# A decoder layer on one core: x loaded once into its final place, cross-attention scores as two halves of 64 rows

## The reference

```
x = ln(x + attn(x))          # one head of width 256 over 1024 tokens, 2 sequences
x = ln(x + xattn(x, ctx))    # 16 heads of width 16, 64 context tokens a sequence, masked and causal
x = ln(x + moe(x))           # 16 experts of width 512, the best 4 of each token
attn:  q, k, v = split(x @ qkv_w.T + qkv_b);  softmax(q @ k.T / 16) @ v @ out_w.T + out_b
xattn: Q, K, V = heads(x @ Wq.T), heads(ctx @ Wk.T), heads(ctx @ Wv.T)
       s = Q @ K.T / 4;  s = -10000 where masked or key > query;  softmax(s) @ V @ Wo.T
```

## Time and profile before

| | us |
|---|---|
| median of 3 runs (657.33 to 663.16) | 661.78 |
| profiled execution | 660.32 |
| its span | 658.5 |

### The profile page before, as it was taken

How to read it: one execution, slowest core, us unless ns; L and a number is a source line. 1 busy time by engine, 2 the same in 40 slices (tenths; PEclk the granted TensorE clock), 3 DMA queues, 4 the chain that set the end, 5 groups by cost and what they waited for, 6 DMA issues and landing times.

```text
span 658.5 us, 14325 instructions
## 1 busy us (share of the span) xinstructions
PE 574.8 (87%) x3996; PEld 513.2 (78%) x3996; DVE 436.9 (66%) x1069; ACT 350.2 (53%) x635; POOL 289.7 (44%) x258
## 2 busy tenths in 40 slices
PE   5899999999789999999658999999999999999800
PEld 4787888888657777777537998999899989999800
DVE  2275555555456777777555778788878877778426
ACT  2263333333234555555321777787777777777605
POOL 5360111111110254555660065766576675667634
PEclk9699999999899999999655899999999999999955
DMA  6189999940000011112229599999999998999477
GB/s 182 34 283 397 397 397 398 397 141 0 1 0 1 26 61 59 68 65 72 82 98 319 162 254 260 217 251 241 257 232 251 251 246 225 247 247 242 77 170 245
DMA packets 91659, 124.36 MB, mean 189 GB/s; under 512 B 6608, under 2 KB 62816, under 8 KB 91632
## 3 DMA queue, kind: packets, MB, share of 16 engines
q1 hardware_dynamic: 73504, 102.26, 47.1%
q0 software_dynamic: 14592, 19.41, 15.5%
q10 hardware_dynamic: 3536, 2.37, 1.2%
HBM read 61.88 MB, written 62.14 MB: 188 GB/s over the span
## 4 chain that ended last, share of the span: by engine, by line
PE 52%; DMA 13%; issue 12%; DVE 10%; SPq 5%; ACT 4%; POOL 2%; DVEq 0%; POOLq 0%; ACTq 0%
PE ps L348 10%; PE ps L350 9%; PE ps L349 9%; DMA xg<-expert_rows 5%; PE ps L756 5%; DMA w1f<-in_L_ffn_w 5%; PE ps L774 4%; PE ps L764 2%; PE ps L790 2%; DVE w_l L1431 2%; PE ps L757 2%; PE ps L740 2%; PE ps L706 2%; DMA expert_sum<-yb,home_row 2%; SPq L388 2%
## 5 line engine op out<-in xcount | busy, mean ns | idle before, releaser
L560 POOL DMA_INDIRECT expert_sum<-yb,home_row x80 | 167.7, 2096 | 116.6 <-DVE home_row L1459 95.7
L348 PE MATMUL ps<-gT_h,w_h 128*128 128x256 f32 x320 | 94.8, 296 | 1.8 <-issue 1.3
L348 PE MATMUL ps<-w_h,h_h 128*128 128x256 f32 x320 | 90.8, 284 | 2.0 <-DVE h_l L1452 2.0
L349 PE MATMUL ps<-gT_l,w_h 128*128 128x256 f32 x320 | 91.4, 286 | 0.0
L350 PE MATMUL ps<-gT_h,w_l 128*128 128x256 f32 x320 | 91.3, 285 | 0.0
L349 PE MATMUL ps<-w_l,h_h 128*128 128x256 f32 x320 | 90.6, 283 | 0.0
L350 PE MATMUL ps<-w_h,h_l 128*128 128x256 f32 x320 | 90.5, 283 | 0.0
L1074 ACT ACTIVATE hf<-ps,b1s 128x256 f32<-128x256 f32 x160 | 62.8, 477 | 38.0 <-PE ps L350 37.9
L541 POOL DMA_INDIRECT expert_rows<-xd,idx x64 | 62.6, 979 | 34.3 <-issue 23.5
L1452 DVE TENSOR_TENSOR h_l<-hf,h_h 128x1024 fp32r<-128x1024 f32 x40 | 49.0, 1225 | 35.7 <-ACT h_h L1081 34.7
L348 PEld LDWEIGHTS ps<-gT_h,w_h 128*128 128x128 f32 x320 | 62.1, 194 | 2.4 <-issue 1.5
(11 more groups left out here) (241 smaller groups left out, 1418.3 us busy)
## 6 DMA issues: line engine op xcount, KB each, us to landing
expert_rows<-zeros SPq DMA_DIRECT2D x32, 1088.0 KB, 14.0
w1f<-in_L_ffn_w SPq DMA_DIRECT2D x40, 512.0 KB
w2f<-in_L_ffn_w SPq DMA_DIRECT2D x40, 512.0 KB, 4.1
xg<-expert_rows SPq DMA_DIRECT2D x40, 272.0 KB
total<-expert_sum SPq DMA_DIRECT2D x16, 256.0 KB, 6.0
expert_sum<-zeros SPq DMA_DIRECT2D x1, 2304.0 KB, 16.1
x_in<-in_x SPq DMA_DIRECT2D x8, 256.0 KB, 2.8
expert_sum<-x_all ACTq DMA_DIRECT2D x8, 256.0 KB
```

What stands on the lines that cost most here:

```text
L348: pe.matmul(o, ah, bh, start=first, stop=False)
L349: pe.matmul(o, ah, bl, start=False, stop=False)
L560: pool.indirect_dma_start(out=sums[p], out_offset=bass.IndirectOffsetOnAxis(ap=home_row[:, p, c:c + 1], axis=0), in_=yb[:, p, c], in_offse ...
```

## The change

The x rows go straight to `x_all`, all eight pairs without a wait, and PE turns them from there; POOL adds `vo` in place. `qkv_w` is loaded in two parts, q and k first, then the first pair of x, then v. `sT_h` and `sT_l` are gone: the value matmuls read `xT_h` and `xT_l`, so ACT and DVE write each part once. PE turns pairs 0 and 1 between the weight products, makes the bias products, and starts the values; turning the cross weights and the context, and the cross keys and values, come after the values of pairs 2, 3, 4 and 5, with the copies on ACT and DVE in the same places. The router's weights and `b2` are loaded by SP behind the context. In the cross scores each bank now belongs to one half of the 128 rows: the mask is a matmul of 64 rows into each bank, and the scores are four fp32 matmuls of 64 rows by 256 columns. The heads come out in another order, which `SCORED` undoes in `cattend`. Semaphores and the copies' banks follow.

```diff
+HALF = P // 2
+HPT = HPC // 2
 PAIRS = HEADS // 2
+SCORED = [hc * (PAIRS // 2) + r * (HPT // 2) + i for r in range(2) for hc in range(KD) for i in range(HPT // 2)]
...
-        hide = sbe("hide", [1, B, SK])
-        hide_r = sbe("hide_r", [1, B, HPC, SK], F32R)
+        hide = sbe("hide", [P, B, SK])
+        hide_r = sbe("hide_r", [P, B, KD * HPT, SK], F32R)
...
-        x_in = sbe("x_in", [P, 2, 2, D])
...
-        kb = sbe("kb", [P, B * KD, HPC, SK])
+        kb = sbe("kb", [P, B * KD, HPT, SK])
...
-        sT_h, sT_l = sbe("sT_h", [P, 2, KD, 2, P], F32R), sbe("sT_l", [P, 2, KD, 2, P], F32R)
...
-            sp.dma_start(n_qkv[:], qkv_w.rearrange("(k p) c -> p k c", p=P)).then_inc(ld_qkv, 16)
+            sp.dma_start(n_qkv[:, 0:2 * KD], qkv_w[0:2 * D].rearrange("(k p) c -> p k c", p=P)).then_inc(ld_qk, 16)
+
+            def load_x(t):
+                sp.dma_start(x_all[:, 2 * t:2 * t + 2], x_rows[t * 2 * P:(t + 1) * 2 * P, :].rearrange("(a p) d -> p a d", p=P)).then_inc(pair_in[t], 16)
+
+            load_x(0)
+            sp.dma_start(n_qkv[:, 2 * KD:3 * KD], qkv_w[2 * D:3 * D].rearrange("(k p) c -> p k c", p=P)).then_inc(ld_v, 16)
+            for t in range(1, NT // 2):
+                load_x(t)
             for n, w in enumerate((wq, wk, wv, wo)):
                 sp.dma_start(n_x[:, n], w.rearrange("(k p) c -> p k c", p=P)).then_inc(ld_wx, 16)
             sp.dma_start(n_ctx[:], ctx.rearrange("b s d -> (b s) d")).then_inc(ld_wx, 16)
+            sp.dma_start(rb[:], router_b.rearrange("(o e) -> o e", o=1).broadcast_to([P, E])).then_inc(ld_b2, 16)
+            for kc in range(KD):
+                sp.dma_start(rw[:, kc], router_w[kc * P:(kc + 1) * P, :]).then_inc(ld_b2, 16)
+            sp.dma_start(b2s[:], b2).then_inc(ld_b2, 16)
             for s in names:
                 sp.sem_inc(s, BIAS)
-
-            def load_x(t, p, k):
-                sp.wait_ge(xT_ps, freed(t))
-                sp.wait_ge(xres, freed(t))
-                sp.dma_start(x_in[:, p], x_rows[ds(t * 2 * P, 2 * P), :].rearrange("(a p) d -> p a d", p=P)).then_inc(ld_x[p], 16)
-
-            pipeline(sp, NT // 2, [(0, load_x)])
...
-            pool.tensor_scalar(hide[:], keep[0:1], -1.0, -HIDDEN, ALU.add, ALU.mult).then_inc(mask_ok, 1)
+            pool.tensor_scalar(hide[:], keep[:], -1.0, -HIDDEN / HALF, ALU.add, ALU.mult).then_inc(mask_ok, 1)
...
-            def residual(t, p, k):
-                if isinstance(t, int) and t == 0:
-                    pool.wait_ge(c_dve, VO_OK)
-                pool.wait_ge(ld_x[p], 16 * k + 16)
-                pool.tensor_tensor(x_all[:, ds(t * 2, 2), :], x_in[:, p], vo[:].unsqueeze(1).broadcast_to([P, 2, D]), ALU.add).then_inc(xres, 1)
-
-            pipeline(pool, NT // 2, [(0, residual)])
+                pool.tensor_copy(hide_r[:, b], hide[:, b].unsqueeze(1).broadcast_to([P, KD * HPT, SK])).then_inc(mask_ok, 1)
+
+            pool.wait_ge(c_dve, VO_OK)
+            for t in range(NT // 2):
+                pool.wait_ge(xT_ps, t + 1)
+                pool.tensor_tensor(x_all[:, 2 * t:2 * t + 2], x_all[:, 2 * t:2 * t + 2], vo[:].unsqueeze(1).broadcast_to([P, 2, D]), ALU.add).then_inc(xres, 1)
...
-                    kv = kv_step(pool.tensor_tensor(kb[:, b * KD + hc], kt[:, hc, b * SK:(b + 1) * SK].unsqueeze(1).broadcast_to([P, HPC, SK]),
-                                                    blk[:].unsqueeze(2).broadcast_to([P, HPC, SK]), ALU.mult), kv)
+                    for r in range(2):
+                        rows = slice(r * HALF, (r + 1) * HALF)
+                        kv = kv_step(pool.tensor_tensor(kb[rows, b * KD + hc], kt[rows, hc, b * SK:(b + 1) * SK].unsqueeze(1).broadcast_to([HALF, HPT, SK]),
+                                                        blk[rows, r * HPT:(r + 1) * HPT].unsqueeze(2).broadcast_to([HALF, HPT, SK]), ALU.mult), kv)
...
+            def turn_x(t):
+                pe.wait_ge(pair_in[t], 16)
+                if t >= 2:
+                    pe.wait_ge(xTl, t - 1)
+                for kc in range(KD):
+                    for a in range(2):
+                        mm = pe.transpose(ps[:, t % 2, (kc * 2 + a) * P:(kc * 2 + a + 1) * P], x_all[:, 2 * t + a, kc * P:(kc + 1) * P], ident[:])
+                mm.then_inc(xT_ps, 1)
+
+            def values(t):
+                pe.wait_ge(xTh, t + 1)
+                pe.wait_ge(xTl, t + 1)
+                if t >= 2:
+                    pe.wait_ge(vl, t - 1)
+                for a in range(2):
+                    rows = slice((2 * t + a) * P, (2 * t + a + 1) * P)
+                    for kc in range(KD):
+                        mm = mm3(pe, ps[:, 2 + t % 2, a * D:(a + 1) * D], xT_h[:, kc, rows], xT_l[:, kc, rows],
+                                 wvo_h[:, kc], wvo_l[:, kc], kc == 0, kc == KD - 1)
+                mm.then_inc(v_ps, 1)
+
+            def turn_cross_weights():
+                pe.wait_ge(ld_wx, 80)
+                pe.wait_ge(c_dve, VO_OK)
+                for n in range(4):
+                    turn(4 + n, n_x[:, n])
+
+            def turn_context():
+                pe.wait_ge(c_act, 3)
+                for kc in range(KD):
+                    mm = pe.transpose(ps[:, 4, kc * P:(kc + 1) * P], n_ctx[:, kc * P:(kc + 1) * P], ident[:])
+                mm.then_inc(c_pe, 1)
+
+            def cross_keys():
+                pe.wait_ge(c_dve, TURNED_OK)
+                for ko in range(KD):
+                    for ki in range(KD):
+                        mm = pe.matmul(ps[:, 5, ko * P:(ko + 1) * P], wkT[:, ki, ko * P:(ko + 1) * P], cT[:, ki],
+                                       start=ki == 0, stop=ki == KD - 1)
+                mm.then_inc(c_mm, 1)
+
+            def cross_values():
+                pe.wait_ge(c_act, 4)
+                for b in range(B):
+                    for ki in range(KD):
+                        mm = pe.matmul(ps[:, 7, b * D:(b + 1) * D], cT2[:, ki, b].rearrange("p a k -> p (a k)"),
+                                       wvT[:, ki], start=ki == 0, stop=ki == KD - 1)
+                mm.then_inc(c_mm, 1)
+
             pe.wait_ge(ident_ok, 1)
             pe.wait_ge(ld_out, 16)
-            turn(0, n_out)
-            pe.wait_ge(ld_qkv, 16)
+            turn(5, n_out)
+            turn_x(0)
...
+            turn_x(1)
+
+            pe.wait_ge(ld_v, 16)
...
+            pe.wait_ge(c_act, 2)
+            pe.wait_ge(c_dve, WVO_OK)
...
+            for t in range(NT // 2):
+                if t == NT // 2 - 1:
+                    pe.wait_ge(c_dve, TURNED_OK)
                     query_of(0, 0, 0)
-                values(t, p, k)
-                if last:
-                    scores_of(0, 0, 0)
-
-            pipeline(pe, NT // 2, [(0, turn_x), (1, values_and_first)])
-            pe.wait_ge(vl, done(NT // 2 - 1))
-            pe.wait_ge(vh, done(NT // 2 - 1))
-            pe.wait_ge(xTl, done(NT // 2 - 1))
+                values(t)
+                if t + 2 < NT // 2:
+                    turn_x(t + 2)
+                if t == 2:
+                    turn_cross_weights()
+                if t == 3:
+                    turn_context()
+                if t == 4:
+                    cross_keys()
+                if t == 5:
+                    cross_values()
+            pe.wait_ge(c_dve, KT_OK)
+            scores_of(0, 0, 0)
+            pe.wait_ge(vl, NT // 2)
+            pe.wait_ge(vh, NT // 2)
+            pe.wait_ge(c_dve, SETUP_DVE)
+            pe.wait_ge(c_pool, POOL_SETUP)
...
+                for r in range(2):
+                    rows = slice(r * HALF, (r + 1) * HALF)
+                    pe.matmul(ps[:, r], ones_r[rows], hide_r[rows, p].rearrange("p h k -> p (h k)"), start=True, stop=False)
                 for hc in range(KD):
-                    pe.matmul(ps[:, hc], cq[:, p, hc], kb[:, p * KD + hc].rearrange("p h k -> p (h k)"), start=True, stop=False)
-                    mm = pe.matmul(ps[:, hc], ones_r[0:1], hide_r[:, p].rearrange("p h k -> p (h k)"), start=False, stop=True)
+                    for r in range(2):
+                        rows = slice(r * HALF, (r + 1) * HALF)
+                        mm = pe.matmul(ps[:, r, hc * D:(hc + 1) * D], cq[rows, p, hc], kb[rows, p * KD + hc].rearrange("p h k -> p (h k)"),
+                                       start=False, stop=hc == KD - 1)
...
-                for g in range(PAIRS):
-                    mm = pe.matmul(ps[:, 5, g * 2 * VW:(g + 1) * 2 * VW], cpT[:, g], vb[:, p, g], start=True, stop=True)
+                for g, pair in enumerate(SCORED):
+                    mm = pe.matmul(ps[:, 5, pair * 2 * VW:(pair + 1) * 2 * VW], cpT[:, g], vb[:, p, pair], start=True, stop=True)
...
+            def x_high(t):
+                act.wait_ge(xT_ps, t + 1)
+                act.activation(xT_h[:, :, t * 2 * P:(t + 1) * 2 * P], ps[:, t % 2].rearrange("p (k c) -> p k c", k=KD), ACT.Copy).then_inc(xTh, 1)
+
+            def v_high(t):
+                act.wait_ge(v_ps, t + 1)
```

(81 more changed lines are left out.)

95 lines of the change are left out of this document (18 added, 77 removed).

## The result

The changed kernel takes **630.94 us** (median of 5 runs, 628.53 to 640.26) against 661.78 (5 runs, 657.09 to 663.16): 0.956 times the time before, with an interval of 0.952 to 0.960. Later runs on other chips gave 0.961 (0.957 to 0.966) and 0.958 (0.954 to 0.962). The forecast was 640.5. The change brought 31 us in the medians, and 27 and 28 in the two repeats, where 20 had been summed up. The execution of 640.26 is over 1.5% above the fastest of its kernel and is left out of the ratio.

What follows compares the result with a forecast made beforehand. The prediction took PE to set the pace in the cross stage, with DVE next, and PE's own list to bound the setup. From 660.32 us, minus 9.5 (setup) and 10.3 (cross stage), it forecast 640.5, range 630 to 652.

Steps and rivals of the forecast that it cites:

- cross term: Cross stage: shorter score passes save 10.3 us in all, with ends of 4.5 and 13.5.
- rival A: Cross scores: the two halves overlap fully, saving 13.5 us there, total 637.3 us; chance 0.22.
- Setup, 9.5: Setup: PE's list up to the first scores sums to 37.3 us against 46.85, 9.5 us less.
- All in place at about 17: Setup loads: 16 issues without a wait, about 4.4 MB, take 14 us and are in place at about 17.
- The pass, 2.16, between 1.70 and 2.62: Cross scores: a pass falls from 2.94 us to 2.16, the middle between partly overlapping (1.70) and serial (2.62).
- only the second of two and the first of the next two can overlap: Cross scores: issued two by two per half, eight score matmuls take five places of 0.23 us, a pass of 1.70.
- two steps can't fall below 15.5: Cross loop: DVE limits two steps to 15.5 us, from 16.88, a saving of 0.69 a step.
- the 1.05 ahead of `residual2`: Cross loop: DVE loses 1.05 us in every second step, cause unknown, left in as a cost.
- DVE's path, 7.22 a step: Cross stage: from `head_max` to the end of `router_inv`, nothing of PE's holds DVE, 7.22 us a step.
- B: Cross scores: nothing of the two halves overlaps, total 646.3 us; chance 0.13.
- C: Setup: PE waits for a pair or copy after 14 us and its clock falls, total 645.5 us; chance 0.12.
- D: Cross scores: each of ten matmuls pays for the row change, a pass of 3.9 to 5.1, up to 684 us; chance 0.06.

Runs made afterwards that it cites:

- weights_first: Changed kernel with cross weights, context, cross keys and cross values moved ahead of the values of the eight pairs, loads as after; 633.78 us, ratio 0.964.
- halves_apart: Changed kernel with the four score matmuls of one half issued first, then the four of the other; 631.41 us, ratio 0.959.
- setup_only: Changed kernel with the cross scores of the kernel before, so only the new setup remains; 648.21 us, ratio 0.988.
- before_no_mask: Kernel before with the mask matmuls of the cross scores left out; one execution, 642.02 us, 16.6 below the median of before.
- third profile: Profile of a later run of the unedited changed kernel, that execution 628.65 us, near the median.
- one_half: Changed kernel with all matmuls of a scores pass on rows 0 to 63; one execution, 667.22 us against a median of 658.62 for the kernel before.
- first profile: Profile of the changed kernel's execution of 640.26 us, the one left out of the ratio.
- second profile: Profile of the unedited changed kernel run once more, that execution 625.35 us.

## Why the prediction was right, and where its sizes were off

The direction, the place of both gains and the setup were right. The total fell at the low edge of the range because the cross term was sized too small. It lies 0.9 us inside, and the median of one repeat, 629.56, lies just outside. What kept it in are the 7 us below rival A that the prediction left for waits that go as well, and that is in part luck.

- **Setup, 9.5.** Measured 9.7, and 9.7 for this half alone. The terms were right one by one: the start 7.33 (7.67), first value matmul "near 16" (15.60), first scores 37.3 (37.16), full clock from 12 us on, the wait of 0.4 kept, SP's waits gone. "All in place at about 17" held too: in `weights_first` PE's wait for the last load ends at 17.69.
- **The pass, 2.16, between 1.70 and 2.62.** It was 1.30, outside both ends. The step that failed is "only the second of two and the first of the next two can overlap", and with it the middle taken between that and no overlap. `halves_apart` shows that four instructions of one half run beside four of the other. The end should have been all columns of one half, 0.23 + 4 x 0.23 = 1.15, and the changes: the page TensorEngine Tiling (Array Packing) of the Trainium skill, section Key Properties, says that different tiles execute in parallel, without a word on neighbours. The runs agree with it (1.30 on two halves against 2.39 on one).
- **What a pass is worth, "two steps can't fall below 15.5".** They fell to 14.4. The failing step is the 1.05 ahead of `residual2`, kept as a cost because its cause wasn't known; it let a step fall by 0.69, where the measured step fell by 1.24. `setup_only` and `before_no_mask` have no such pause at 8.44 and at 7.21 a step: it was slack. The floor that did come, 7.2, is DVE's wait for the exponential, by the rows the ring over POOL's sends and ACT's buffer. The prediction's own reading of DVE's path, 7.22 a step, is the same size, and it counted the 1.05 on top.
- **The sum again with both mended.** 5 steps ahead of the loop at 1.64, 7 in it at 8.44 - 7.2 = 1.24, two ends at 1.64: 20.2 instead of 10.3, and 660.3 - 9.5 - 20.2 = 630.6. The median is 630.9. By the table the two cross stretches gave 3.1 + 17.4 = 20.5. Term by term it is looser: the seven steps from tile 0 to 7 gave 7.5, the eight behind them 9.9. And of the 3.1 ahead of tile 0 the pass explains 1.64; the rest is clock. Before, the clock was 0.79 over 170 to 178 us, ahead of tile 0. In the third profile it is 0.86 over 176 to 186, behind tile 0, so what the first stretch gained the second lost. That the total meets the median to 0.3 is luck as well, for the medians of before alone lie between 657.8 and 661.8. The 1.8 of the experts, which the change doesn't touch, lie within what two executions of one kernel differ by.
- **The rivals.** A, full overlap, had the mechanism, but its pass was the same 1.70 and its gain was cut off by the same false floor (637.3). B, no overlap, is refuted by `one_half` against the change. C, PE starved in the setup, didn't come; `weights_first` shows what it costs, 4.3 us to the first scores. D, each matmul pays for a change of rows, fell: a pass is 1.30 and not 3.9, and alternating is the quicker of the two orders.

## What to carry to other kernels

Where the rows of a matmul serve separate outputs, as with keys laid on diagonal blocks, split it over the two halves of the rows: here two such matmuls ran side by side in both orders tried, and the two masks took 0.33 together. Before costing a wait as kept, ask whether it could be slack of the engine that sets the pace: add up each engine's own work, and a wait that fills the difference can go with it. And when the pace setter gets 20% shorter, look for rings through buffers (write, send, overwrite) that ran with room before: here one took back 0.4 us a step, and 0.2 of it came back by moving the waiting instruction on the consumer's queue, and nothing by moving the late one on the producer's.

## What the runs showed of the hardware

- Two fp32 matmuls on 64 rows each, on different halves: a pass of 1.30 alternating and 1.41 in fours. On the same half: 2.39.
- A fall of the clock at tile 0 in all three profiles of the changed kernel. PE waits 2.4 to 2.5 us for ACT there, 0.78 before. In the first profile the clock falls behind that wait:

```profile
179.09 1.10 PE L793 MATMUL ps<-ident,prob 128*128 128x128 f32 x8 [2.53 <-ACT prob L1030]
```

```profile
175.00:180.00 5.00, 2.28 (x18) 1.77 (x19) 3.58 (x3) 1.19 (x2) 1.21 (x2) 1.00 0.00 0
180.00:185.00 5.00, 5.00 (x28) 4.87 (x26) 2.49 (x3) 2.46 (x3) 0.37 (x1) 0.55 0.02 3
185.00:190.00 5.00, 5.00 (x22) 3.98 (x23) 3.09 (x4) 0.68 (x2) 0.00 (x0) 0.50 0.00 0
```

PE was busy 2.28 of 5 us, and the clock then fell from full (2.4 GHz) to half (1.2 GHz); two steps took 7.0 and 7.6 us instead of the 5.2 and 6.0 of the second profile, 3.5 us in all. In the third profile the clock falls as PE takes up work again, and the stretch is shorter; the second looks the same:

```profile
175.90 1.97 PE L793 MATMUL ps<-ident,prob 128*128 128x128 f32 x8 [2.40 <-ACT prob L1030]
```

```profile
160.00:176.00 16.00, 9.49 (x71) 7.41 (x70) 9.16 (x16) 3.62 (x6) 3.05 (x5) 0.98 0.00 0
176.00:186.00 10.00, 10.00 (x73) 9.43 (x74) 6.58 (x10) 5.06 (x7) 1.15 (x1) 0.86 0.01 2
```

Before, the clock stayed at 1.00 behind the wait of 0.78 (185 to 192 us). So the longer wait goes with a fall in each profile; what decides how long it lasts was not found. The first profile had been at half clock shortly before too (0.74 over 165 to 175). Its span is 15.0 us longer than the second's, and only 3.5 of that lie in these two steps: 3.6 were lost before tile 0, and 7.9 behind the last `head_max`.
- In `one_half` the clock fell without any idle time: PE was busy for 5.00 of 5.00 us in both windows.

```profile
215.00:220.00 5.00, 5.00 (x38) 4.70 (x37) 4.36 (x26) 3.43 (x6) 1.35 (x2) 1.00 0.00 0
220.00:225.00 5.00, 5.00 (x21) 4.13 (x20) 2.74 (x5) 1.23 (x5) 3.32 (x4) 0.51 0.27 98
```

Over 170 to 304 us its mean clock was 0.85. As an estimate, 0.15 of 134 us is 20 us of full clock lost there, enough to make it slower than the kernel before although its pass is shorter. Why the clock fell was not found.
